# Attention scores with the keys in partitions, and a softmax turned by VectorE, in a gated cross-attention block

## What is computed

```python
x   = x + tanh(g_xattn) * attention(layernorm(x), ctx, ctx)     # x: 4 x 512 x 1024, ctx: 4 x 64 x 1024
x   = x + tanh(g_ffn) * ffn(layernorm(x))
# attention: 32 query heads, 8 key heads of 128, rotary turn of queries and keys
scores = einsum('bhqd,bhkd->bhqk', queries, keys) * 128 ** -0.5
scores = where(tril(ones(512, 64)), scores, finfo.min)
attn   = softmax(scores)
out    = (attn @ values) @ Wd.T
# ffn: rows scaled and rounded to 8 bit, gate and up to 512, silu(gate) * up, rounded again, down to 1024
```

## Time and profile before

| | |
|---|---|
| median of three timed runs | 1485.55 us (1484.33 to 1486.3) |
| the profiled execution's own time | 1490.73 us |
| its span in the trace | 1488.9 us |
| TensorE busy | 1431.8 us, 96% of the span |
| DVE, ACT, POOL busy | 1005.5, 563.2, 614.7 us (68, 38, 41%) |
| the chain that ended last | 79% on PE, 12% on DVE |
| granted TensorE clock, mean | 0.993 |

### The profile page before, as it was taken

One profiled execution on the slowest core, in us unless ns is written; L12 is line 12 of the kernel. 1 busy time (PEld: TensorE's weight loads), 2 busy tenths in 40 slices (PEclk: granted clock), 3 DMA queues, 4 the chain that ended last, 5 costly groups with the idle time before them and its releaser, 6 DMA issues.

```text
span 1488.9 us, 19163 instructions
## 1 busy us (share of the span) xinstructions
PE 1431.8 (96%) x7248; PEld 1169.9 (79%) x7248; DVE 1005.5 (68%) x1563; ACT 563.2 (38%) x864; POOL 614.7 (41%) x429
## 2 busy tenths in 40 slices
PE   7999999999999999999999999999999999997887
PEld 7878888888888888887878888888888888874443
DVE  5866575757576766667475757566666666677997
ACT  4424141414242323244542423232322323147995
POOL 3435242434343343440343433434433434233784
PEclk9999999999999999999999999999999999998999
DMA  8834343433425243437265242433333334464565
GB/s 296 251 95 107 72 114 72 106 88 82 112 64 119 68 106 80 108 78 238 74 177 137 70 107 61 95 76 94 83 89 86 94 72 108 93 206 148 120 128 99
DMA packets 327131, 166.52 MB, mean 112 GB/s; under 512 B 275200, under 2 KB 290048, under 8 KB 326656
## 3 DMA queue, kind: packets, MB, share of 16 engines
q1 hardware_dynamic: 324448, 154.29, 39.0%
q0 software_dynamic: 2592, 11.01, 4.5%
HBM read 132.74 MB, written 35.65 MB: 113 GB/s over the span
## 4 chain that ended last, share of the span: by engine, by line
PE 79%; DVE 12%; ACT 3%; DMA 2%; issue 2%; POOL 2%; SPq 1%; ACTq 0%; POOLq 0%; DVEq 0%
PE psum L561 16%; PE psum L563 16%; PE psum L562 16%; PE psum L615 8%; PE psum L650 7%; PE psum L652 7%; PE psum L651 7%; DVE psum L1625 2%; DVE vw_lo L1354 1%; DVE res L1672 1%; DMA acc<-in_x 1%; DMA wv_raw<-in_wv_t 1%; DVE xg L1635 1%; POOL rot L1239 1%; DVE pt_lo L1354 1%
## 5 line engine op out<-in xcount | busy, mean ns | idle before, releaser
L561 PE MATMUL psum<-xt_hi,wq_hi 128*128 128x512 f32 x1024 | 402.1, 393 | 2.6 <-DVE xt_lo L1354 2.6
L562 PE MATMUL psum<-xt_lo,wq_hi 128*128 128x512 f32 x1024 | 399.7, 390 | 0.0
L563 PE MATMUL psum<-xt_hi,wq_lo 128*128 128x512 f32 x1024 | 399.7, 390 | 0.0
L1211 POOL TENSOR_TENSOR wq_lo<-wq_raw,wq_hi 128x512 fp32r<-128x512 f32 x128 | 170.0, 1340 | 490.7 <-ACT wq_hi L918 490.7
L1515 DVE TENSOR_TENSOR acc<-psum,acc 128x512 f32<-128x512 f32 x224 | 151.3, 681 | 140.3 <-PE psum L652 140.3
L1239 POOL TENSOR_TENSOR rot<-rot 128x1024 f32<-128x1024 f32 x64 | 153.5, 2399 | 207.8 <-DVE rot L1458 207.0
L561 PEld LDWEIGHTS psum<-xt_hi,wq_hi 128*128 128x128 f32 x1024 | 193.1, 189 | 42.2 <-DVE xt_lo L1354 2.8
L563 PEld LDWEIGHTS psum<-xt_hi,wq_lo 128*128 128x128 f32 x1024 | 192.9, 188 | 40.8
L964 ACT ACTIVATE vw_hi<-psum 64x512 fp32r<-64x512 f32 x256 | 151.4, 591 | 194.0 <-PE psum L563 190.3
L562 PEld LDWEIGHTS psum<-xt_lo,wq_hi 128*128 128x128 f32 x1024 | 192.9, 188 | 39.5
L1354 DVE TENSOR_TENSOR vw_lo<-psum,vw_hi 64x512 fp32r<-64x512 f32 x256 | 175.4, 686 | 52.9 <-ACT vw_hi L964 46.8
(11 more groups left out here) (151 smaller groups left out, 1915.8 us busy)
## 6 DMA issues: line engine op xcount, KB each, us to landing
wq_raw<-in_wq_t SPq DMA_DIRECT2D x128, 256.0 KB, 4.4
wd_raw<-in_wd_t SPq DMA_DIRECT2D x128, 256.0 KB, 3.6
p_scratch<-prob SPq DMA_DIRECT2D x60, 256.0 KB, 2.0
pt_raw<-p_scratch SPq DMA_DIRECT2D x240, 64.0 KB, 2.5
acc<-in_x SPq DMA_DIRECT2D x16, 512.0 KB, 5.5
out_x<-acc SPq DMA_DIRECT2D x16, 512.0 KB, 3.9
xa<-out_x SPq DMA_DIRECT2D x16, 512.0 KB, 3.6
out_x<-res POOLq DMA_DIRECT2D x15, 512.0 KB, 5.5
```

The source lines that it names most:

```text
L561: pe.matmul(dst, a_hi, b_hi, start=start, stop=False)
L562: pe.matmul(dst, a_hi, b_lo, start=False, stop=False)
L563: return pe.matmul(dst, a_lo, b_hi, start=False, stop=stop)
L1211: pool.tensor_tensor(dst, full, hi.bitcast(F32), ALU.subtract).then_inc(done, 1)
```

## The change

Scores have the keys in partitions now (2 heads x 64 keys by 512 queries), from keys and turned queries that are both split in high and low parts; the softmax works on blocks of 32 x 32 that VectorE transposes out of PSUM, and nothing of the probabilities goes through memory. With 32 keys in a block, the maximum and the sum of 64 keys are put together with the neighbour block, which lies in other partitions: `other_half` copies four pieces of 32 partitions.

```diff
 def score(unit):
-    for t in range(BT):
-        for j in range(2):
-            pe.matmul(scores[:, t*P:(t+1)*P], rot[:, 0, j, t*P:(t+1)*P], kblk[:, j, 2*b:2*b+2, :], ...)
+    pe.wait_ge(rot_lo_done, unit + 1)
+    for j in range(2):
+        ins = three(scores, keys_hi, keys_lo, rot_hi[:, j, :], rot_lo[:, j, :], j == 0, j == 1)
...
+def copy_turned(unit):       # ACT
+    act.wait_ge(rope_done, unit + 1)
+    act.activation(rot_hi[:, :, :], rot[:, 0, :, :], ACT.Copy).then_inc(rot_hi_done, 1)
+def lower_turned(unit):      # POOL
+    pool.wait_ge(rot_hi_done, unit + 1)
+    lower(rot_lo[:, :, :], rot[:, 0, :, :], rot_hi[:, :, :], rot_lo_done)
 def add_turned(unit):        # POOL
-    pool.tensor_tensor(rot[:, 0, :, :], rot[:, 0, :, :], rot[:, 1, :, :], ALU.add)
+    pool.tensor_tensor(rot[:, 0, 0, :], rot[:, 0, 0, :], rot[:, 1, 1, :], ALU.subtract)
+    pool.tensor_tensor(rot[:, 0, 1, :], rot[:, 0, 1, :], rot[:, 1, 0, :], ALU.add)
...
+def other_half(part, done):  # DVE
+    for a in range(4):
+        ins = dve.tensor_copy(other[32*(a^1):32*(a^1)+32, part // 2, :], tops[32*a:32*a+32, part, :])
 def softmax_a(unit):         # mask on 64 columns, transpose out of PSUM, maximum of 32
+    dve.transpose(prob[:, :, :], blocks(scores))
+    dve.tensor_reduce(tops[:, 0, :], prob[:, :, :], AX_X, ALU.max)
+def softmax_less(unit):      # other_half(0), maximum of the two, subtract
 def softmax_b(unit):         # sum of 32, other_half(2), add, reciprocal, times the gate
+def softmax_c(unit):         # times that, and transpose into pt_raw
...
 DVE, kind == 0 and filled:
+    turn_second(unit - 1)
+    softmax_b(unit - 2)
+    softmax_c(unit - 2)
+    lower_values(gg - 1, 5)
+    lower_values(gg - 1, 6)
+    lower_probs(unit - 2)
+    lower_values(gg - 1, 7)
+    softmax_a(unit - 1)
+    softmax_less(unit - 1)
+    turn_first(unit)
+    add(gg - 1, 0)
+    softmax_b(unit - 1)
+    softmax_c(unit - 1)
+    add(gg - 1, 1)
 DVE, kind == 1 and not filled:
     turn_second(unit - 1)
     softmax_a(unit - 1)
     turn_first(unit)
+    softmax_less(unit - 1)
     softmax_b(unit - 1)
+    softmax_c(unit - 1)
```

More of the change, by code:

```diff
@@ L47 @@
 BT = SEQ // P
+TB = SEQ // 32
 UPG = 2 * HB
@@ L674, in slot @@
                         outputs(gg - 1, 0)
+                        score(unit - 1)
                     else:
@@ L700, in slot @@
                     queries(unit, 6)
+                    if not filled:
+                        score(unit - 1)
                     queries(unit, 7)
@@ L816, in last_outputs @@
                     turn_rows(1, 0)
-                for c in range(3, 8):
+                outputs(gg - 1, 3)
+                score(unit - 1)
+                for c in range(4, 8):
                     outputs(gg - 1, c)
-                turn_probs(unit - 1)
                 if half == 0:
                     turn_rows(1, 1)
+                    turn_rows(1, 2)
                 outputs(gg - 1, 8)
                 outputs(gg - 1, 9)
-                if half == 0:
-                    turn_rows(1, 2)
                 outputs(gg - 1, 10)
@@ L1004, in slot @@
                     copy_probs(unit - 2)
-                    exponential(unit - 1)
+                    copy_turned(unit - 1)
+                    if filled:
+                        exponential(unit - 1)
                     copy_values(gg, 0)
@@ new lines, in slot @@
+                if kind == 0 and not filled:
+                    for t in range(BT, BT + 2):
+                        lower_rows(half, t)
+                    turn_first(unit)
+                    for t in range(BT + 2, HTILES):
+                        lower_rows(half, t)
+                if kind == 1 and filled:
+                    turn_second(unit - 1)
+                    add(gg - 1, 2)
+                    lower_probs(unit - 2)
+                    add(gg - 1, 3)
+                    add(gg - 1, 4)
+                    softmax_a(unit - 1)
+                    softmax_less(unit - 1)
+                    turn_first(unit)
+                    add(gg - 1, 5)
+                    softmax_b(unit - 1)
+                    softmax_c(unit - 1)
+                    add(gg - 1, 6)
+                    add(gg - 1, 7)
@@ L1561, in slot @@
+                if kind == 1 and not filled:
+                    turn_second(unit - 1)
                     softmax_a(unit - 1)
                     turn_first(unit)
-                    if filled:
-                        lower_probs(unit - 2)
-                        add(gg - 1, 5)
+                    softmax_less(unit - 1)
                     softmax_b(unit - 1)
-                    if filled:
-                        add(gg - 1, 6)
-                        add(gg - 1, 7)
-                    if half == 0:
-                        dve.wait_ge(xs_in, 16 * (u // UPG + 1))
-                        statistics(HTILES + u // UPG, xn[:, :])
@@ L1579, in slot @@
+                if kind == 2 and not filled:
+                    turn_second(unit - 1)
+                    lower_probs(unit - 2)
+                    lower_values(gg, 0)
                     softmax_a(unit - 1)
                     turn_first(unit)
-                    if filled:
-                        add(gg - 1, 11)
+                    softmax_less(unit - 1)
                     softmax_b(unit - 1)
-                    if filled:
-                        add(gg - 1, 12)
-                    else:
-                        lower_probs(unit - 2)
```

409 lines of the change are left out of this document (210 added, 199 removed).

## The result

The changed kernel takes 1597.27 us (median of 4 executions, 1592.34 to 1598.62), the kernel before 1485.92 beside it. The direction was right, the size was not.

A forecast was written before the change was run, and what follows sets the result against it. TensorE's own work was taken to bound the filled groups, so savings and new waits count in full. Terms -29.4 - 1.7 + 51.8 - 2.7 + 27.9 - 5 + 5 - 2.6 + 0 = +43.3 on 1485.6 gave 1529 us, range 1470 to 1562.

The forecast's parts named there:

- 14 x (3.7 - 1.84) - 2.7: Filled groups: 3.7 us of new waits each, 1.84 saved by cheaper scores; 2.7 us of today's second-half loss goes.
- 27.9 - 5: First groups of both halves: new waits add 27.9 us (22 to 32); today's two `vw_lo` waits go, 5 us.
- 5 - 1.7: Ends of halves: longer chain between twelve adds costs 5 us (0 to 10); removed `turn_probs` transposes save 1.7.
- The three waits: TensorE in a filled group, at `turn_first`, `add(1)` and the score of kind 1: 3.3 us in all.
- The first rival: Filled groups: VectorE's idle time takes the new work, no waits come, giving 1462 us; chance 0.17.
- the second: Whole kernel: waits come, but unknown terms lie near or below their low ends, 1478 to 1496 us; chance 0.13.
- the 0.4 for `lower_values(5)`: Kind 0 of a filled group: `values(7)` waits 0.4 us more, as this step now follows a sum and a transposition.
- a wait was held for covered: Kinds 2 and 3 of filled groups: the chain ends before TensorE comes, no wait, 0.5 to 1.5 us to spare.
- The waits of 13.35: First group of a half: TensorE's waits over kinds 1 to 3 and the first filled slot sum to 13.35 us.
- The -2.6: Prologue: TensorE's wait for `xt_lo` ends since `lower_rows(0, 3)` comes before the statistics; -2.6 us (-2.6 to 0).
- -9 to +6: Feed-forward: range around 0, ACT's passes cut at the start but added to four steps, square root done twice.
- The third rival: VectorE and POOL disturb each other on SBUF, stretching POOL's chain steps by 1.4, about 3 us per group: 1570 us; chance 0.08.

The follow-up runs named there:

- softmax_last: Changed kernel with VectorE's softmax sum and what follows it moved behind `turn_second` in kinds 0 and 1 of filled groups, nothing left out; 1537.09 us.
- add1_early: Changed kernel with one VectorE step moved: in kind 0 of a filled group `add(1)` comes ahead of the softmax sum and the rest; 1587.98 us.
- wd_first: Changed kernel with the split of the output weights taken ahead in the queues of ACT and POOL, nothing else; 1572.52 us.
- side_undone: Changed kernel with the edits beside the scores undone (statistics of tiles 6 and 7, down columns' scaling, second normalisation in one piece); 1586.09 us.
- ends_too: Reordered kernel without the side edits, with the ends of halves reordered too and `rstd` and `shift` operations in the last kind 3; 1490.73 us.

## Why the prediction was right, and why wrong

By stage, forecast and measured (profiled executions), in both cuts. The forecast's terms by stage: 14 x (3.7 - 1.84) - 2.7; 27.9 - 5 and six scores; 5 - 1.7 and two scores, a score being 0.46 us less:

| stage | forecast | cut at `queries(u, 0)` | cut at `turn_first` |
|---|---|---|---|
| 14 filled groups (measured: 54 of 56 slots) | +23.3 | +49.1 | +41.0 |
| first groups | +20.1 | +36.1 | +40.7 |
| ends | +2.4 | +13.4 | +12.5 |
| prologue | -2.6 | -3.1 | +1.4 |
| feed-forward | 0 | +6.1 | +6.1 |

By the cut at `queries(u, 0)` the 58 us between +43.3 and the 101.6 of the profiled executions are 26 in the filled slots, 16 in the first groups, 11 at the ends and 6 in the feed-forward part. No single term makes them.

**The chain, right.** The three waits (forecast 0.8 for `turn_first`, 2.1 for `add(1)`, 0.4 for the score) came as 0.56, 1.76 and 0.35 us of idle time. The product behind each is 0.16 us late, as in the forecast, and the next one another 0.11 (0.08 in the score), which the forecast had not counted: 3.45 us where 3.3 were forecast. The durations taken by bounds came as chosen: a set of copies 0.72 (0.76 forecast, 0.171 us each), the transposition out of PSUM 0.717 (0.71), the mask 0.228 (0.23):

```profile
L1486 DVE COPY other<-psum 32x16 f32<-32x16 f32 x512 | 87.4, 171 | 9.5
L1494 DVE STREAM_TRANSPOSE prob<-psum 128x512 f32<-128x512 f32 x64 | 45.9, 717 | 2.2
```

softmax_last shows that the waits were that chain, add1_early that they are one. The first rival (no waits) and the second fall.

**The filled groups, mis-sized.** A group takes 81.6 us in the first half and not 79.9. In one (units 16 to 19, 81.62 us) I laid each product's distance to the one before beside 0.2269, the distance before the change. (1) The wait for `wd_lo` comes twice, 0.60 us in kind 0 and 0.21 in kind 3, each with 0.27 of taking up: 1.35 us, in place of the 0.4 for `lower_values(5)`, which TensorE, late by then, no longer met. I had moved each queue's new steps past DVE's work but not past the split weights in ACT's and POOL's queues, although `split_wd` stands between `add_turned` and `lower_turned` in the change. This is the step that failed: the chain was laid out on DVE's queue alone of three, and kind 3, where a wait was held for covered, has one. (2) The score costs more than 6 x 0.227 = 1.36: 1.41 us in kinds 0 and 3 (its products stand 0.233 apart), and 1.56 in kind 2, where the first comes 0.09 late and the second 0.08; 0.3 a group. (3) The other products stand 0.2274 apart instead of 0.2269, 0.2 a group. With the 0.15 of the chain this is 1.6 of the 1.7 us that are missing. The largest part, 0.95 us for `wd_lo`, is 13 us over the filled slots.

**The first groups, mis-sized twice.** The waits of 13.35 came out near that in sum (14.9 and 14.6 of idle time), but that is luck. In the first half the places that the forecast named make 5.8 us (1.6 and 2.0 for `turn_first` and `turn_second`, 2.2 for `rot_lo`), and the others 9.1: 7.9 for `wd_lo`, which was not in the list, and 1.2 for `wq_lo`. The exponential in ACT's queue waits 7.4 us with the next weights behind it. The second miss is the clock: 13 and 10 us at half of it against 3 and 0 before. TensorE at half clock starts a product every 0.43 us instead of 0.23, so some 20 us more of it cost up to 10 us. wd_first shows what it is worth: the first group fell by 6.3 us, of which only 2.4 are idle time; its granted clock rose from 0.92 to 0.98. The forecast had no term for the clock, although the trace of before shows the same thing at a wait of 2.1 us (below). The cut at `queries(u, 0)` also has the wait of 4.3 us for `far` in the first group.

**Ends, prologue, feed-forward.** The range of 0 to +10 for the ends was too small: with the two scores and the small turns it ends at +7.4, and 12.5 to 13.4 were measured. In the first of them TensorE's waits rose from 3.8 us to 11.6 (8.3 for `add`, 3.3 for `vw_lo`), and the clock was at half for 6.8 us of it; the forecast had not laid this chain out. The prologue and the feed-forward part were counted as -2.6 and 0. The -2.6 came, up to the first product of `queries(0, 0)`, but the wait for `far` stood right behind it; side_undone gives -2.3 and -7.0 when the edits are undone. In the feed-forward part the normalisation now stands at step 3, beside POOL, and two of its operations on 4 columns take 1.25 and 1.01 us. That the range there (-9 to +6) was so wide shows that nothing was known of it; the middle was a guess.

**The third rival, half right.** DVE and POOL do disturb each other: `pt_lo` takes 1.60 us on average, 0.98 before. But POOL's steps on the chain took what was laid out, so the chain was not stretched by 1.4 as this rival had it, and no part of the account of a filled group is put down to it:

```profile
L1217 POOL TENSOR_TENSOR rot_lo<-rot,rot_hi 128x1024 fp32r<-128x1024 f32 x64 | 153.4, 2397 | 21.1 <-ACT rot_hi L964 21.1
L1376 DVE TENSOR_TENSOR pt_lo<-pt_raw,pt_hi 128x512 fp32r<-128x512 f32 x64 | 102.5, 1601 | 79.9 <-ACT pt_hi L945 79.5
```

It costs where small operations stand on a path: ends_too shows it for the end of a half, and in the kernel after the `far` rows and the two operations of the feed-forward part are such places, though no run took POOL's work alone away from them.

**Medians.** The rest between 101.6 and 111: the three other executions of the kernel after have granted clocks of 0.973, 0.973 and 0.976 and spans of 1594.3, 1596.6 and 1596.8 us, the profiled one 0.980 and 1590.5. A kernel that waits often has more half clock, and not the same in each execution.

## What to carry to other kernels

When a step gets longer or is moved, lay out its chain on every queue that it passes, and list for each queue what stands behind the new waits: here DVE's was laid out to 0.1 us, while the wait of 5 us came from weights that stood behind an exponential on ACT, and shorter ones from weights behind additions on POOL. Of a chain, only its length counts; taking one stop off it moves the wait on, and what helps is to put first what TensorE waits for (turn, add, split weights) and last what nobody does (the softmax). A change that brings work to an engine with a third of its time idle is not lost when it first comes out 7% slower: the same scores and softmax in another order, without the edits beside them, gave 0.9% less than before. And cut two kernels at events that stand at the same place of the busiest engine's list, or work moves between the stages that are compared.

## What the runs showed of the hardware

Small DVE operations on SBUF are held by POOL. One of 8 columns took 0.17 to 0.23 us alone and 1.04 to 1.22 us beside POOL's subtractions, and ended with POOL's; `pt_lo` (337.31 to 339.83) ended 0.55 us after the `rot_lo` (336.88 to 339.28) that it met. The other way round POOL is held: `wq_lo` at 658.12 met a running `pt_lo` and took 1.74 us instead of 1.29. The ends that fall together look like a lock for a whole instruction rather than a shared rate. The Trainium skill, "SBUF — State Buffer", section "SBUF: two separate sides", says that: the pair of ports that VectorE and GpSimd share is held by whichever starts first for its whole instruction, and the other fully blocks, where VectorE's operation has two SBUF inputs or runs in a 2-port perf mode. By that rule a small operation costs as much as POOL's instruction has left, and the trace agrees (0.02 or 0.03 us between the two ends, five times). The RECIPROCAL, with one input, was not held: 0.19 us at 658.62, 0.20 at 632.26, both with a POOL instruction running. The TENSOR_SCALAR at 661.16 also reads one tensor and was held; whether it ran in that mode no run here shows. The forecast took the factor of 1.4 from the rows for a stretch of both.

TensorE's clock fell at waits that are short: before the change already, for 3.4 us behind one of 2.09 us (108.77), and in the kernel after behind one of 2.22 us (112.26), behind one of 2.17 (129.05) and within the one of 5.15 (136.40 to 141.55). The two windows of the kernel after on either side of this last fall, at 139.70:

```profile
132.80:139.70 6.90, 3.60 (x16) 2.63 (x14) 5.93 (x13) 0.69 (x2) 1.48 (x2) 0.99 0.12 41
139.70:146.50 6.80, 4.95 (x12) 3.89 (x13) 2.08 (x3) 3.86 (x7) 3.77 (x3) 0.50 0.12 40
```

In the filled slots, with four or five waits of 0.2 to 1.8 us in a group, it mostly stays up (1.00), but at 863.3, behind the wait of 1.78 us for `add(1)` in the first filled group of the second half, it fell for 3.4 us, and in the execution of side_undone it fell three times in the first 27 slots (0.99 over 554 us): some 10 us at half clock without any other wait than in the kernel after. There a group with such a fall takes 82.4 us or more, one without 81.4 to 81.6.
